# Second attention: maxima written negated by their reduction, and its input parts made at other places

## The reference

```
x = x + tanh(g_xattn[0]) * L0_xattn(layernorm(x), ctx)        # one head
x = x + tanh(g_ffn[0])   * L0_ffn(layernorm(x))               # routed low-rank adapter
x = x + tanh(g_xattn[1]) * L1_xattn(ctx, ctx, layernorm(x))   # 16 heads of 16
x = x + tanh(g_ffn[1])   * L1_ffn(layernorm(x))               # 16-head self attention, two token classes
```

## Time and profile before

| what | us |
|---|---|
| median of 3 runs | 1404.75 |
| the profiled execution | 1407.3 |
| its span | 1405.6 |
| PE busy in it | 1242.0 (88%) |
| DVE busy | 1047.9 (75%) |
| ACT busy | 856.5 (61%) |
| GpSimd busy | 160.4 (11%) |

### The profile page before, as it was taken

How to read it: one execution, slowest core, us unless ns; L and a number is a source line. 1 busy time by engine, 2 the same in 40 slices (tenths; PEclk the granted TensorE clock), 3 DMA queues, 4 the chain that set the end, 5 groups by cost and what they waited for, 6 DMA issues and landing times.

```text
span 1405.6 us, 26286 instructions
## 1 busy us (share of the span) xinstructions
PE 1242.0 (88%) x10562; PEld 579.1 (41%) x10562; DVE 1047.9 (75%) x1563; ACT 856.5 (61%) x1432; POOL 160.4 (11%) x139
## 2 busy tenths in 40 slices
PE   4888973889899899947899999999999999999978
PEld 3566661444456755513333333233323232323337
DVE  4896594667664756546799999999999999999802
ACT  2233472667574255501488887787887888877871
POOL 2220022221600223312400000000000000000000
PEclk8977985999889999979899999999999999999999
DMA  5100026355450023332432444332444432443003
GB/s 179 25 1 14 1 30 112 79 76 117 96 86 1 0 90 135 132 78 31 72 68 53 72 83 73 61 65 53 81 82 68 62 65 55 83 82 48 2 2 120
DMA packets 78824, 92.54 MB, mean 66 GB/s; under 512 B 15210, under 2 KB 53356, under 8 KB 78704
## 3 DMA queue, kind: packets, MB, share of 16 engines
q1 hardware_dynamic: 78704, 90.87, 32.3%
HBM read 67.02 MB, written 23.80 MB: 65 GB/s over the span
## 4 chain that ended last, share of the span: by engine, by line
PE 56%; DVE 30%; ACT 7%; issue 3%; DMA 1%; SPq 1%; POOL 1%; DVEq 0%; ACTq 0%; POOLq 0%
DVE sm L1961 18%; PE ps L1451 9%; PE ps L1442 9%; PE ps L1423 6%; PE ps L1342 4%; ACT W L958 3%; PE ps L1561 2%; PE ps L1161 2%; PE ps L1349 2%; PE ps L1241 2%; PE ps L1232 2%; PE ps L1233 2%; PE ps L1290 2%; PE ps L1433 1%; DVE XN L1594 1%
## 5 line engine op out<-in xcount | busy, mean ns | idle before, releaser
L1961 DVE TENSOR_REDUCE sm<-ps 128x1 f32<-128x1024 f32 x512 | 599.8, 1218 | 31.5 <-PE ps L1423 28.2
L958 ACT ACTIVATE W<-ps 128x512 f32<-128x512 f32 x1024 | 534.7, 604 | 138.3 <-PE ps L1451 134.4
L1451 PE MATMUL ps<-R 99*32 99x512 bf16 x4096 | 317.8, 383 | 6.2 <-ACT W L958 3.2
L1442 PE MATMUL ps<-W,R 128*32 128x512 f32 x2048 | 265.3, 594 | 0.7 <-ACT W L958 0.7
L1451 PEld LDWEIGHTS ps<-R 99*32 99x32 bf16 x4096 | 86.0, 94 | 224.8 <-ACT W L958 168.6
L1423 PE MATMUL ps<-R 50*128 50x512 bf16 x512 | 88.9, 388 | 15.4 <-DVE sm L1961 12.7
L1423 PE MATMUL ps<-KM,R 50*128 50x512 bf16 x512 | 87.2, 384 | 9.6 <-DVE sm L1961 6.6
L876 ACT CAST R<-ps 4x2048 bf16<-4x2048 f32 x32 | 59.5, 1858 | 57.5 <-PE ps L1212 57.5
L889 ACT ACTIVATE R<-ps 77x512 f32<-77x512 f32 x128 | 71.4, 592 | 23.0 <-PE ps L1233 20.3
L1767 DVE TENSOR_REDUCE small<-ps 128x4 f32<-128x308 f32 x128 | 57.8, 473 | 36.4 <-PE ps L1199 36.2
L1442 PEld LDWEIGHTS ps<-W,R 128*32 128x32 f32 x2048 | 63.0, 111 | 42.2 <-ACT W L958 1.4
(11 more groups left out here) (258 smaller groups left out, 1542.2 us busy)
## 6 DMA issues: line engine op xcount, KB each, us to landing
R<-x_parts SPq DMA_DIRECT2D x96, 128.0 KB, 5.0
R<-q_parts SPq DMA_DIRECT2D x192, 64.0 KB
R<-q_parts SPq DMA_DIRECT2D x96, 128.0 KB
R<-k_parts SPq DMA_DIRECT2D x96, 128.0 KB
x_parts<-R SPq DMA_DIRECT2D x8, 768.0 KB, 6.9
q_parts<-R SPq DMA_DIRECT2D x24, 256.0 KB, 2.6
k_parts<-R SPq DMA_DIRECT2D x24, 256.0 KB, 2.6
X<-in_x SPq DMA_DIRECT2D x4, 1024.0 KB, 9.9
```

The source lines that it names most:

```text
L958: act.activation(PR[:, s % 2, h, :], third_bank("score", 64 * u + n), ACT.Exp, scale=0.25).then_inc(s_sfree, 1)
L1442: mm = pe.matmul(bank(7)[32 * h:32 * h + 32, :], VST[j][:, k, h, :], PR[:, s % 2, h, :], start=(k == 0), stop=(k == TB - 1))
L1451: mm = pe.matmul(o[32 * c:32 * c + 32, :], KST[j][0:MAX_ROW + 1, h, t:t + 32], QST[j][0:MAX_ROW + 1, h, 512 * (s // 8):512 * (s // 8) + 51 ...
L1961: dve.tensor_reduce(MX[:, half, h, q:q + 1], bank(2 * ((p + 1) % 2), 2), AX, ALU.max).then_inc(s_tfree, 1)
```

## The change

Three things are changed, all in the second attention:
- the reductions write their maxima negated and in bf16, directly to Mn; the tensor_scalar, M1 and the semaphore between them are gone. PE's transposes wait for the fourth reduction of the half unit, and DVE waits for a free buffer Mn ahead of the reductions;
- FIRST is 8: halves 4 to 7 are made ahead of the loop too (banks 0 to 3 again), and chunks 2 and 3 are normalised there. In the loop halves 8 to 15 are made in m = 2, 4, ..., 16, and chunks 4 to 7 are normalised in m = 0, 3, 7, 11;
- SP writes chunks 2 and 3 after the load of stack 2, chunks 4, 5, 6, 7 after those of stacks 5, 7, 9, 11.

```
-        FIRST = 4
-        HALVES = {max(0, 8 * (i // 4) - 2) + i % 4: FIRST + i for i in range(12)}
-        CHUNKS = {0: 3, 4: 4, 6: 5, 12: 6, 14: 7}
+        FIRST = 8
+        HALVES = {2 * i + 2: FIRST + i for i in range(8)}
+        CHUNKS = {0: 4, 3: 5, 7: 6, 11: 7}
+        WRITES = {2: (2, 3), 5: (4,), 7: (5,), 9: (6,), 11: (7,)}
...   SP
                 load_x_stack(u)
-                if u % 4 == 3 and b + 1 < B:
-                    write_parts(2 * b + 2)
-                    write_parts(2 * b + 3)
+                for c in WRITES.get(u, ()):
+                    write_parts(c)
...   ACT
-            for n in range(FIRST):
+            for n in range(4):
                 part_h(n, bank(n))
                 if n >= 1:
                     part_m(n - 1)
-            part_m(FIRST - 1)
+            part_m(3)
             act.wait_ge(s_v1, 1)
             act.wait_ge(s_v1m, 2)
             for j in range(2):
                 act.copy(V1a[:, :, 8 * j:8 * j + 8, 0:D],
                          bank(4 + j)[0:KX, :].rearrange("p (b h d) -> p b h d", b=B, h=8)).then_inc(s_v1c, 1)
+            for n in range(4, FIRST):
+                part_h(n, bank(n % 4))
+                if n >= 5:
+                    part_m(n - 1)
+            part_m(FIRST - 1)
...   PE
             for n in range(FIRST):
-                transpose_half(n, bank(n))
+                if n >= 4:
+                    pe.wait_ge(s_pr, n - 3)
+                transpose_half(n, bank(n % 4))
...
             def max_transposes1(m):
-                pe.wait_ge(s_mn, m + 1)
+                pe.wait_ge(s_mr, 4 * m + 4)
...   DVE
-            for n in range(FIRST):
+            for n in range(4):
                 residue(n, bank(n))
...
-            ln_chunks(2, [2], lambda c: None)
+            ln_chunks(2, [2, 3], lambda c: None)
+            for n in range(4, FIRST):
+                residue(n, bank(n % 4))
...
-                    dve.tensor_reduce(M1[:, u % 2, q, :],
+                    dve.tensor_reduce(Mn[:, u % 2, q, :],
                                       bank(n % 2)[:, 0:4 * KX].rearrange("p (j n) -> p j n", j=4), AX,
-                                      ALU.max).then_inc(s_mr, 1)
+                                      ALU.max, negate=True).then_inc(s_mr, 1)

             def maxima1(m, between=lambda: None):
                 u, v = m // 2, slice(4 * (m % 2), 4 * (m % 2) + 4)
+                if m >= 4:
+                    dve.wait_ge(s_mt, m - 3)
                 reduce1(u, range(v.start, v.start + 2))
                 between()
                 reduce1(u, range(v.start + 2, v.stop))
-                if m >= 4:
-                    dve.wait_ge(s_mt, m - 3)
-                dve.wait_ge(s_mr, 4 * m + 4)
-                dve.tensor_scalar(Mn[:, u % 2, v], M1[:, u % 2, v], -1.0, None, ALU.mult).then_inc(s_mn, 1)
```

More of the change, by code:

```diff
@@ L221, in build_program @@
         OnT = R3f[:, 0:2048].rearrange("p (u j n) -> p u j n", u=2, j=2)
-        M1 = small[:, 400:464].rearrange("p (u q j) -> p u q j", u=2, q=8)
         Mn = small[:, 464:496].bitcast(BF16).rearrange("p (u q j) -> p u q j", u=2, q=8)
@@ L244, in build_program @@
         s_mr = sem("max1_reduced")
-        s_mn = sem("max1_negated")
         s_mt = sem("max1_transposed")
```

## The result

| | median, us | runs |
|---|---|---|
| before | 1405.51 | 1402.43 to 1411.99 (4) |
| after | 1370.47 | 1368.27 to 1372.99 (4) |

The ratio of the runs is 0.9745, 95% interval 0.9706 to 0.9784: 35 us less, where 38.7 less (1366) was forecast. The profiled execution took 1368.27 us (before 1407.3), its span 1366.5.

What follows compares the result with a forecast made beforehand. PE bounds the kernel, busy 88% of the span, so only its waits or low-clock stretches give time back. 33.0, 5.2 and 0.45 sum to 38.7 less: 1407.3 to 1368.6, or 1366 on the median's scale; range 1361 to 1379.

Steps and rivals of the forecast that it cites:

- m=2 to 29: Second attention's loop: 5 half units at 5.42, 3 at 5.78, 20 at 4.68; 171.05 becomes 138.04, 33.0 us less.
- m=0 and 1: First two half units of the second attention's loop: 12.97 us becomes 7.75, 5.2 less.
- two negations ahead of the loop: Two negations removed before the loop, 0.17 us and their hand-over, 0.22 each: 0.45 us less.
- ahead of the maxima: Extra chunk and halves made before the loop lie under the first stack's transfer: cost 0, at most 9 us uncovered.
- The half units: In the loop, 6.57 us with a part (transposes, copy, residue of half a chunk) becomes 5.42; behind a chunk 5.78.
- The bounds of 5.18 and 6.57: Half unit with a part: 5.18 us if no wait is left, 6.57 if nothing is gained.
- The stop at m=20: Negation held 4.75 us under GpSimd's bias addition to X, then clock 0.50; m=20 to 23 get 13.75 us shorter.
- Rival C: Loop reductions are held by GpSimd in the negation's place: some 32 us in all, 1398 us; chance 0.03.
- Rival D: Negated reduction is slow, DVE bounds plain half units: at 1.4 us each some 57 more, 1423 us; chance 0.03.
- Writes and stacks: SP's queue in the loop: moved writes cost 0; stack 12 is tightest, with 0.5 to 1.7 us to spare.
- Rival E: Stack 12 or 8 comes late, PE waits some 2 us at m=22: 1368 to 1378 us; chance 0.09.
- m=6: Half unit where PE waits for batch 1's stack because writes and loads came late: 10.47 us becomes 5.42.

Runs made afterwards that it cites:

- part 1 alone: Kernel before with only the negation taken into the reductions (negated bf16 output), parts and writes left in place; 1383.25 us, ratio 0.9784.
- without the additions: Kernel before with GpSimd adding the bias to 16 columns of one tile per batch instead of all of X; 1394.66 us, ratio 0.9858.
- the other kind of negation: Kernel before with the negation made by a negated tensor_reduce over a one-element dimension instead of the tensor_scalar; 1384.9 us, ratio 0.9788.
- Part 2 alone: Changed kernel with the negation put back (fp32 maxima into M1, then the tensor_scalar and its semaphore); 1390.01 us, ratio 0.9834.
- late writes: Changed kernel with chunks 2 and 3, 4 and 5, 6 and 7 written behind the loads of stacks 3, 7, 11; 1397.73 us against 1372.39.

## Why the prediction was right

| term | forecast, us less | measured |
|---|---|---|
| m=2 to 29 | 33.0 (to 138.04) | 33.2 (to 137.87) |
| m=0 and 1 | 5.2 | 5.0 |
| two negations ahead of the loop | 0.45 | 0.4 |
| warm-up matmuls | none | 1.4 |
| ahead of the maxima | 0 | 1.1 |
| behind the loop | 0 | -2.0 |
| sum | 38.7 | 39.1 (span) |

The mechanism came as forecast, and nearly all of the gain with it. Two things in the table are luck. The 1.4 and 1.1 us ahead of the loop are how this execution fell out: the sixteen warm-up matmuls took 4.76 us in it and 4.90 and 6.22 in the changed kernel's other two traces (6.17 before), and PE's first maxima tile started at 230.89, 232.39 and 231.44 (231.98 before). The 2.0 us behind the loop happen to cancel most of that.

- **The half units.** With a part 5.42 was forecast and 5.40 came, behind a chunk 5.78 and 5.78. The reading that the negation ends them, and that PE's slot for the values is next, was right; part 1 alone shows it. The bounds of 5.18 and 6.57 were not needed.
- **The stop at m=20.** 13.8 us, as forecast; the runs without the additions and with the other kind of negation each remove it on their own. The second one also shows that the kind of instruction makes it, where the prediction had inferred GpSimd's hold from two ends 0.03 us apart. The size of the stop hangs on timing, which the prediction did not say. Two more negations of before fell under the additions:

```profile
363.35 0.42 DVE L1779 TENSOR_SCALAR small<-small 128x16 bf16<-128x16 f32 x1
368.02 0.23 DVE L1779 TENSOR_SCALAR small<-small 128x16 bf16<-128x16 f32 x1
```

Each addition takes 4.5 us, so the four end near 363.7, 368.2, 372.7 and 377.2. The first two negations met the end of an addition and cost nothing; the third (372.69) met the fourth addition just begun (372.6) and lasted beyond its end (377.44). Part 2 alone repeats the three (0.41, 0.23 and 4.77 us), since there too the additions start right behind a half unit with a part. Rival C (the reductions are held instead) is refuted by sixteen reductions under the additions at 0.45 us each.

- **Rival D**, a slow negated form: 0.85 for two, no change.
- **Writes and stacks.** No stack was waited for. Rival E did not come, and the margin for stack 12 was enough (its load starts at 340.96, and PE first uses it at 351.53, 10.6 us later). Part 1 alone, with the writes at their old places, does wait for that stack, 0.5 us in m=22. What the prediction had not seen is how much hangs on the writes' places: it priced late loads, and the run with late writes shows that the buffer PB is the sharper limit, 24.6 us in the loop.
- **m=6.** The prediction put the whole of 10.47 minus 5.42 down to the late stack. In four traces in which the parts are made and written at the places of before, PE's wait is 2.21, 1.89, 0.77 and 2.91 us, and the half unit takes 10.47, 8.80, 7.13 and 9.81. Against the run without the additions, the luckiest of them, 1.4 us were a longer wait and 1.9 the clock's fall; with the 1.3 of m=3 the kernel before had, in the profiled execution, up to 4.7 us of ill luck that the sum counted as gain. It was counted rightly for that execution.
- **Median against trace.** The trace gave 39.1 us of span and the medians 35.0. The sum was made for one profiled execution and then carried over to a median of others. Most of the time that isn't steady lies in two places: the waits and stops in the loop of before, and the stretch behind the projections that the kernel's code calls the register queries (the five extra rows of the self attention). From its first matmul (line 1378 of before) to the last of line 1395 it takes 66.3 us in part 2 alone, 66.8 before, 66.7, 66.7 and 69.7 in the changed kernel's traces, and 69.8 to 72.7 in the others. There the mean clock over 54 us was 0.94 in one trace and 0.84 in another (part 2 alone, then part 1 alone):

```profile
612.29:666.29 54.00, 42.41 (x255) 22.94 (x253) 36.89 (x48) 8.53 (x12) 24.92 (x6) 0.94 0.41 57
```

```profile
598.29:652.29 54.00, 43.33 (x232) 25.28 (x232) 33.19 (x42) 7.37 (x10) 20.56 (x6) 0.84 0.31 46
```

The changed kernel's profiled execution was the fastest of its four, and the one of before lay above its median; that is why the difference of the two spans is larger than that of the medians. Whether the change itself makes the part behind the loop longer stays open: 977.9, 978.1 and 979.5 us in its three traces, 976.0 in the one of before, 974.5 in part 2 alone and up to 983.6 in others. One piece of it splits the traces cleanly: from the self attention's first matmul of line 1442 (1447 in after) to the end of the span it is 715.1 us before and 715.2 in part 2 alone, and 718.0 to 718.5 in the eleven others, with a mean clock of 0.98 and 0.97 over its first 30 us against 0.92 in the changed kernel, in part 1 alone and without the additions. The two short ones are the traces with the stop at m=20; no run shows whether that is more than chance.

## What to carry to other kernels

When the same tiny instruction takes now 0.17 and now 1.06 or 4.75 us, suspect that another engine holds it: compare its end with the ends of GpSimd's instructions, and try another kind of instruction for the same work before moving the work (one line was worth 26.8 us here). Such a hold lasts as long as what is left of the other engine's instruction, so one long instruction can cost nothing or all of its length, by timing alone (0.23, 0.42 and 4.75 us here). A stop of a few microseconds on PE can cost twice its length again in the clock (4.0 us of stop and some 9.6 behind it here), so price a stop with the stretch behind it, as a range. When a producer's order is changed, ask for each transfer which buffer it sets free, not only who reads what it brings.

## What the runs showed of the hardware

- A tensor_scalar of 128x16 from SBUF to SBUF waits for the end of GpSimd's instruction in progress (0.17 us free, 1.06 under a subtraction, 0.42, 0.23 and 4.75 under three of the additions), a tensor_reduce of the same data never did (169 to 171 ns, 32 times).
- A reduction that negates and writes bf16 costs the same as one that writes fp32: 473 ns in the mean over 128 of them, before and after.
- With a stop of 4 to 5.5 us the granted clock fell to 0.50 and stayed there for the 14 to 20 us of work behind the stop, PE busy throughout, in the kernel before, in part 2 alone and with late writes (twice). Behind a wait of 1.2 us it fell in m=2 of before and stayed at 1.00 in m=8 of before and in m=2 without the additions; behind the waits of 1.89, 2.21 and 2.91 us in m=6 it fell each time, behind that of 0.77 it did not. In these cases it was back within 3 to 7 us.
- Warm-up matmuls in PE's gaps, most of them single, kept it at 1.00 through the 12.2 us of the maxima and m=0, where ten of them ahead of that stretch didn't: there it fell at 236 and came back at 256.7.
